# An edge-matrix builder: half-width one-hot products in the inner loop, and weighted copies on GpSimd in fewer, wider operations

## The reference, cut to what matters

```python
h = relu(layernorm(x)); x = x + sage(h, src, dst)          # mean over incoming edges, two convolutions
h = relu(layernorm(x)); x = x + gcn(h, edge_weight, ...)    # weighted sum over incoming edges
h = relu(layernorm(x)); x = x + interaction(h, edge_attr)   # sum over incoming edges, layer norm, three-layer MLP
h = relu(layernorm(x)); x = x + maxk(h, ...)                # top 32 of 256 features, mean over incoming edges
```

## Time and profile before

| | |
|---|---|
| median of 3 runs | 1709.41 us (1706.76 to 1711.73) |
| the profiled execution: time, span | 1709.9 us, 1708.1 us |
| granted TensorE clock over the span | 0.971 of full speed |
| busy over the span: PE, DVE, ACT, POOL | 93%, 56%, 37%, 19% |

### The profile page before, as it was taken

How to read it: one execution, slowest core, us unless ns; L and a number is a source line. 1 busy time by engine, 2 the same in 40 slices (tenths; PEclk the granted TensorE clock), 3 DMA queues, 4 the chain that set the end, 5 groups by cost and what they waited for, 6 DMA issues and landing times.

```text
span 1708.1 us, 41810 instructions
## 1 busy us (share of the span) xinstructions
PE 1587.9 (93%) x11011; PEld 1227.7 (72%) x11012; DVE 960.3 (56%) x2841; ACT 625.3 (37%) x1718; POOL 326.2 (19%) x926
## 2 busy tenths in 40 slices
PE   2899999999988999899999999999899999977996
PEld 1555565555666777588878888888778888855885
DVE  5788888888842222233336666666537777773111
ACT  6677787777721111111112222222234444430000
POOL 1565565655610000000000000000011111110000
PEclk8899999999999999999999999999999999988998
DMA  4266676757696666333355655566322212211444
GB/s 133 70 179 170 156 193 164 186 155 195 163 255 202 193 193 194 127 120 130 122 161 155 178 160 159 163 179 174 108 82 80 76 64 80 80 39 62 150 153 152
DMA packets 353541, 245.55 MB, mean 144 GB/s; under 512 B 195243, under 2 KB 337383, under 8 KB 353511
## 3 DMA queue, kind: packets, MB, share of 16 engines
q1 hardware_dynamic: 353510, 245.19, 50.1%
HBM read 138.17 MB, written 99.31 MB: 139 GB/s over the span
## 4 chain that ended last, share of the span: by engine, by line
issue 60%; PE 33%; DVE 3%; POOL 2%; DVEq 1%; SPq 0%; POOLq 0%; DMA 0%; ACT 0%
PE ps L1377 21%; PE ps L1466 8%; POOL work L643 2%; PE ps L1420 1%; PE ps L1418 1%; DVE e_buf L997 0%; DVE work L943 0%; PE ps L1412 0%; PE ps L1639 0%; SPq L419 0%; PE ps L1353 0%; DVE small L1253 0%; PE ps L1365 0%; DVE e_buf L1013 0%; PE ps L1370 0%
## 5 line engine op out<-in xcount | busy, mean ns | idle before, releaser
L1466 PE MATMUL ps<-arena 128*128 128x256 f16 (+1 forms) x5000 | 605.3, 274 | 18.3 <-DVE arena L1317 8.9
L1466 PEld LDWEIGHTS ps<-arena 128*128 128x128 f16 x5000 | 488.1, 98 | 115.5 <-issue 47.2
L1377 PE MATMUL ps<-e_buf 128*128 128x400 bf16 (+1 forms) x2476 | 374.8, 308 | 23.6 <-DVE e_buf L997 23.5
L1377 PEld LDWEIGHTS ps<-e_buf 128*128 128x128 bf16 x2476 | 217.6, 98 | 169.6 <-DVE e_buf L997 51.6
L1460 PE MATMUL ps<-arena 128*128 128x256 f32 x1250 | 279.6, 381 | 0.6 <-ACT arena L791 0.6
L1460 PEld LDWEIGHTS ps<-arena 128*128 128x128 f32 x1250 | 236.5, 191 | 32.3 <-ACT arena L791 0.9
L628 POOL TENSOR_SCALAR e_buf<-e_buf,w_col 128x128 bf16<-128x128 bf16 x600 | 220.9, 382 | 162.5 <-DVE e_buf L993 156.1
L643 POOL TENSOR_TENSOR work<-work 128x256 f32<-128x256 f32 x75 | 54.4, 726 | 1000.7 <-ACT work L836 1000.7
L997 DVE TENSOR_SCALAR e_buf<-iota,off_g,front 128x400 bf16<-128x400 f16 (+1 forms) x619 | 222.3, 405 | 35.0 <-PE ps L1377 30.6
L993 DVE TENSOR_SCALAR e_buf<-iota,front 128x128 bf16<-128x128 f16 x419 | 111.4, 273 | 40.5 <-PE ps L1377 26.8
L669 ACT ACTIVATE e_buf<-e_buf,front 128x128 bf16<-128x128 bf16 x219 | 88.3, 403 | 106.8 <-DVE e_buf L993 106.4
(11 more groups left out here) (214 smaller groups left out, 1580.4 us busy)
## 6 DMA issues: line engine op xcount, KB each, us to landing
arena<-turned_blocks SPq DMA_DIRECT2D x75, 800.0 KB, 4.3
wgt_blocks<-arena SPq DMA_DIRECT2D x25, 1600.0 KB, 10.3
arena<-wgt_blocks SPq DMA_DIRECT2D x25, 1600.0 KB, 8.3
cnt_blocks<-work SPq DMA_DIRECT2D x25, 800.0 KB, 5.6
turned_blocks<-arena SPq DMA_DIRECT2D x25, 800.0 KB, 3.5
e_raw<-edge_features_padded SPq DMA_DIRECT2D x25, 576.0 KB, 7.8
edge_features_padded<-in_edge_attr SPq DMA_DIRECT2D x24, 512.0 KB, 9.9
out<-arena SPq DMA_DIRECT2D x24, 128.0 KB
```

The costliest lines, as they stand in the source:

```text
L1377: return pe.matmul(bank[:, 0:wide], rows_, cols, start=start, stop=True, skip_group_check=True)
L1466: m = pe.matmul(agg[par][:, 0:wide], BLK16[par][:, b * P:(b + 1) * P], ZH[zin(i)][:, b * ZW + part * D:b * ZW + part * D + wide], start=(b ...
```

## The change

The loop over remaining tiles goes over pairs of a tile and a half of the columns (`halves`). The table holds where a group's range begins and ends in such pairs, and whether the first remaining tile reaches only into the second half (`only_b`); if so, the loop goes in steps of two, over second halves alone, otherwise over both halves of each tile. A pass multiplies 200 columns. Its set and its Q stand in a ring of four slots that turns with every pass (`slot_of`), so that VectorE may be three passes ahead; slot, tile and half are computed from the pass's number. The set kept for the next group is found in the same way (`kept`).

GpSimd makes the three weighted copies of a middle set by one `tensor_tensor` of 128 x 384, a set read three times, times three factors that are spread over 128 columns each; the copy to `w_col` and the drain fall away. It also walks the loop over remaining tiles and makes their third weighted copy with a `tensor_tensor` of 128 x 128; ScalarE makes only the second. Four operations are added to the table's computation.

```diff
-RINGW = (Q_AT + 2 * HW + 4 * GW + 1) // 2
+RINGW = (Q_AT + 2 * HW + 2 * GW + SLOTS * HW + 1) // 2
...
-PREP_STEPS = PREP_SCAN + 8 * 1 + 17 + 3
+PREP_STEPS = PREP_SCAN + 10 + 19 + 3
...
+        ring_rest = ring[:, REST_AT:REST_AT + SLOTS * SETS].rearrange("p (s a n) -> p s a n", a=4, n=P)
+        ring_q = ring[:, Q_AT + 2 * HW + 2 * GW:Q_AT + 2 * HW + 2 * GW + SLOTS * HW].rearrange("p (s n) -> p s n", n=HW)
...
-        def rest_set(i, part):
-
-            at = REST_AT + i % SLOTS * SETS + part * P
-            return ring[:, at:at + P]
+        def next_sets(par, part, many):
+
+            at = par * SETS + part * P
+            return ring[:, at:at + many * P]
+
+        def rest_set(slot, part):
+
+            return ring_rest[:, slot, part, :] if isinstance(slot, int) else \
+                ring_rest[:, bass.ds(slot, 1), part, :].rearrange("p o n -> p (o n)")
...
-        def q_rest(par):
-            at = Q_AT + 2 * HW + (2 + par) * GW
-            return ring[:, at:at + GW]
+        def q_rest(slot):
+            return ring_q[:, bass.ds(slot, 1), :].rearrange("p o n -> p (o n)")
+
+        def slot_of(e, k):
+            return e.snap(k & (SLOTS - 1), min_val=0, max_val=SLOTS - 1)
+
+        def tile_of(e, it):
+            return bounded(e.snap(it >> 1), 0, ET)
+
+        def half_of(e, it):
+            return bounded(e.snap((it & 1) * HW), 0, HW)
...
-        def end_of(e, v):
-            return bounded(e.snap(v & 511), 1, ET + 1)
+        def halves(e, v):
+
+            lo = bounded(e.snap(v >> 10), 0, 2 * ET + 1)
+            hi = bounded(e.snap(v & 1023), 2, 2 * ET + 2)
+            by = bounded(e.snap((lo & 1) + 1), 1, 2)
+            return e.Fori(lo, hi, by)
...
-            def weigh_pair(c, i, v):
+            def weigh_pair(c, i, rest, v):
                 n, par = c * PER + i, i % 2
-                w = w_col[:, par, :]
-                pool.tensor_copy(w, col[:, C_W0:C_W2 + 1, bass.ds(low_of(pool, v), 1)].rearrange("p a o -> p (a o)"))
-                pool.drain()
+                factors = col[:, C_W0:C_W2 + 1, bass.ds(low_of(pool, v), 1)].broadcast_to([P, 3, P])
+                plain = next_set(par, 0).rearrange("p (o n) -> p o n", o=1).broadcast_to([P, 3, P])
                 wait(pool, s_hotS, n + 1)
                 pool.sem_inc(s_made, 1)
-                for k in range(3):
-                    m = pool.tensor_scalar(next_set(par, k + 1), next_set(par, 0), w[:, k:k + 1], 1.0,
-                                           ALU.mult, ALU.mult)
-                m.then_inc(s_hotP, 1)
-
+                pool.tensor_tensor(next_sets(par, 1, 3).rearrange("p (a n) -> p a n", n=P), plain, factors, ALU.mult
+                                   ).then_inc(s_hotP, 1)
+                k_reg = step_of[mybir.EngineType.Pool]
+                with halves(pool, rest) as it:
+                    k = pool.snap(k_reg, min_val=0, max_val=1 << 20)
+                    t, slot = tile_of(pool, it), slot_of(pool, k)
+                    wait(pool, s_restS, k + 1)
+                    pool.tensor_tensor(rest_set(slot, 3), rest_set(slot, 0), one(col[:, C_W2, :], t).broadcast_to([P, P]),
+                                       ALU.mult).then_inc(s_restP, 1)
+                    pool.reg_add(k_reg, k_reg, 1)
...
-                packed = pairs_of(pool, mybir.EngineType.Pool, c, "fixed")
+                packed = pairs_of(pool, mybir.EngineType.Pool, c, "both")
                 for i in range(PER):
-                    weigh_pair(c, i, packed[i])
+                    weigh_pair(c, i, packed[i], packed[PER + i])
...
-                with act.Fori(high_of(act, v), end_of(act, v)) as t:
+                with halves(act, v) as it:
                     k = act.snap(k_reg, min_val=0, max_val=1 << 20)
+                    t, slot = tile_of(act, it), slot_of(act, k)
                     wait(act, s_restS, k + 1)
-                    act.activation(rest_set(i, 2), rest_set(i, 0), ACT.Copy, scale=one(col[:, C_W1, :], t))
-                    act.activation(rest_set(i, 3), rest_set(i, 0), ACT.Copy,
-                                   scale=one(col[:, C_W2, :], t)).then_inc(s_restA, 1)
+                    act.activation(rest_set(slot, 2), rest_set(slot, 0), ACT.Copy, scale=one(col[:, C_W1, :], t)
+                                   ).then_inc(s_restA, 1)
                     act.reg_add(k_reg, k_reg, 1)
...
+                tiles_under(last_a[:, o], 1, 2 * nb, ALU.is_le)
...
-            chain(dve.tensor_scalar(end, last, 1.0, None, ALU.add))
-            chain(dve.scalar_tensor_tensor(out=pair, in0=rest, scalar=512.0, in1=end, op0=ALU.mult, op1=ALU.add))
+            chain(dve.tensor_tensor(only_b, rest, last_a, ALU.is_gt))
+            chain(dve.scalar_tensor_tensor(out=begin, in0=rest, scalar=2.0, in1=only_b, op0=ALU.mult, op1=ALU.add))
+            chain(dve.tensor_scalar(end, last, 2.0, 2.0, ALU.mult, ALU.add))
+            chain(dve.scalar_tensor_tensor(out=pair, in0=begin, scalar=1024.0, in1=end, op0=ALU.mult, op1=ALU.add))
...
-                dve.reg_add(room, k_reg, 1)
-                with dve.Fori(high_of(dve, v), end_of(dve, v)) as t:
-                    wait(dve, s_restused, dve.snap(room, min_val=1, max_val=1 << 20))
-                    edge_rows(rest_set(i, 0), t, s_restS)
-                    dve.tensor_scalar(rest_set(i, 1), iota1[:, 0:P], one(col[:, C_S, :], t), one(col[:, C_W0, :], t),
-                                      ALU.is_equal, ALU.mult)
-                    edge_cols(n, q_rest(par), GW, t, s_restQ)
+                with halves(dve, v) as it:
+                    k = dve.snap(k_reg, min_val=0, max_val=1 << 20)
+                    t, slot = tile_of(dve, it), slot_of(dve, k)
+                    wait(dve, s_restused, k + 1)
+                    edge_rows(rest_set(slot, 0), t, s_restS)
+                    dve.tensor_scalar(rest_set(slot, 1), iota1[:, 0:P], one(col[:, C_S, :], t),
+                                      one(col[:, C_W0, :], t), ALU.is_equal, ALU.mult)
+                    edge_cols(n, q_rest(slot), HW, t, s_restQ, at=half_of(dve, it))
                     dve.reg_add(k_reg, k_reg, 1)
-                    dve.reg_add(room, k_reg, 2)
                 edge_cols(n, q_next(par), GW, u, s_hotQ)
...
-            pe.sem_inc(s_restused, 2)
+            pe.sem_inc(s_restused, SLOTS - 1)
...
+                kept = slot_of(pe, pe.snap(k_reg, min_val=0, max_val=1 << 20) + (SLOTS - 1))
                 wait(pe, s_taken, n + 1)
                 wait(pe, s_hotQ, n * 2 + 1)
-                product(counts, HW, rest_set(i - 1, 0), q_first(par), start=True)
-                product(weights, HW, rest_set(i - 1, 1), q_first(par), start=True)
-                product(weights, HW, rest_set(i - 1, 2), q_first(par))
-                product(weights, HW, rest_set(i - 1, 3), q_first(par)).then_inc(s_used, 1)
-
-                with pe.Fori(high_of(pe, v), end_of(pe, v)):
+                product(counts[:, 0:HW], rest_set(kept, 0), q_first(par), start=True)
+                product(weights[:, 0:HW], rest_set(kept, 1), q_first(par), start=True)
+                product(weights[:, 0:HW], rest_set(kept, 2), q_first(par))
+                product(weights[:, 0:HW], rest_set(kept, 3), q_first(par)).then_inc(s_used, 1)
+
+                with halves(pe, v) as it:
                     k = pe.snap(k_reg, min_val=0, max_val=1 << 20)
+                    slot, at = slot_of(pe, k), half_of(pe, it)
                     wait(pe, s_restQ, k + 1)
-                    product(counts, GW, rest_set(i, 0), q_rest(par))
-                    product(weights, GW, rest_set(i, 1), q_rest(par))
+                    product(span(counts, at, HW), rest_set(slot, 0), q_rest(slot))
+                    product(span(weights, at, HW), rest_set(slot, 1), q_rest(slot))
                     wait(pe, s_restA, k + 1)
-                    product(weights, GW, rest_set(i, 2), q_rest(par))
-                    product(weights, GW, rest_set(i, 3), q_rest(par)).then_inc(s_restused, 1)
+                    product(span(weights, at, HW), rest_set(slot, 2), q_rest(slot))
+                    wait(pe, s_restP, k + 1)
+                    product(span(weights, at, HW), rest_set(slot, 3), q_rest(slot)).then_inc(s_restused, 1)
                     pe.reg_add(k_reg, k_reg, 1)
 
                 wait(pe, s_hotQ, n * 2 + 2)
-                product(counts, GW, next_set(par, 0), q_next(par))
+                product(counts[:, 0:GW], next_set(par, 0), q_next(par))
                 wait(pe, s_hotP, n + 1)
-                product(weights, GW, next_set(par, 1), q_next(par))
-                product(weights, GW, next_set(par, 2), q_next(par))
-                product(weights, GW, next_set(par, 3), q_next(par)).then_inc(s_used, 1)
+                product(weights[:, 0:GW], next_set(par, 1), q_next(par))
+                product(weights[:, 0:GW], next_set(par, 2), q_next(par))
+                product(weights[:, 0:GW], next_set(par, 3), q_next(par)).then_inc(s_used, 1)
```

(2 more changed lines are left out.)

18 lines of the change are left out of this document (9 added, 9 removed).

## The result

The changed kernel takes 1984.5 us (median of 4 runs, 1982.9 to 1987.0), the kernel before 1708.1 (4 runs, 1705.3 to 1711.7): 1.162 times as long, 95% interval 1.159 to 1.165. That is 276 us more; 204 were forecast. The profiled execution has a span of 1985.2 us.

What follows compares the result with a forecast made beforehand. The prediction took TensorE's columns and VectorE's instruction stream to bound the build, and TensorE's register steps to bound it after the change. Its sum was 1709.9 + 202 (build) + 2 (table) = 1914 us, range 1840 to 1990.

Steps and rivals of the forecast that it cites:

- What bounds the kernel before: In the build, 426 of 1708 us, TensorE's columns (1.72 us a group) and VectorE's instruction stream were both at the limit.
- whatever the operations take: VectorE in the build: its sequencer needs 1.5 to 1.7 us a group, however long its operations last.
- the busy shares do not show it: In the build, VectorE runs at TensorE's pace, 1.73 us a group, which busy shares were said to hide.
- TensorE's steps decide: In the changed build, TensorE's register steps set the pace: 628 us for 426, +202 us; chance 0.54.
- 24 x 0.10 + 0.1 ... = 2.5 us: TensorE's group in the changed build: 24 register steps at 0.10 us, plus 0.1 for branch and matmuls' hand-over.
- up to 50 ns more, 0.4 us: Upper end for TensorE's eight matmuls a group with addresses in registers: up to 50 ns more each, 0.4 us.
- The estimate of 17 ns a step: TensorE's register steps priced by the skill's issue floor: 24 would take 0.4 us, hidden under columns; the prediction set it aside.
- VectorE, 572 us: VectorE in the changed build: 20 steps and six operations a group at 86 ns; 572 us, below TensorE's 628; rival's chance 0.20.
- 1.0 to 1.1 and 0.36 us: GpSimd's new operations: 384 columns in 0.96 to 1.09 us, a pass's 128 in 0.32 to 0.36, hidden; rival's chance 0.07.
- VectorE's operations get no longer in sum: VectorE in the build: 200 instead of 400 columns saves 0.1 us a pass; 32 more passes cost 0.6 each.
- The clock: Rival: TensorE's clock falls to 1.2 GHz throughout the build, +254 + 2, 1966 us; chance 0.12.
- The columns: TensorE's loop streams 149,600 columns less, 64 us; rival where columns decide: 1648 us, chance 0.05.

Runs made afterwards that it cites:

- the two loops: Kernel before, with a table flag sending second-half-only groups to a second copy of TensorE's loop, 200 columns wide at fixed addresses: 1704.5 us, 0.997.
- the first experiment: Kernel before, with TensorE reading the same remaining-tile sets at addresses computed from its own counter, 20 register steps a group instead of 8: 1816.9 us, 1.064.

## Why the prediction was right, and where its sizes were off

*What bounds the kernel before: right in the main.* TensorE's columns and VectorE at one pace is what the two loops showed: 64 us of columns less, and the build's end moves by 0.2 us. More steps on TensorE alone slow it too. That VectorE's pace there is its steps, "whatever the operations take", is not shown. In the stretch of the earlier trace rows, by the columns of the earlier trace rows, its operations fill 5.08 of 5.20 us:

```profile
293.40:298.60 5.20, 5.20 (x37) 3.12 (x36) 5.08 (x19) 4.96 (x15) 3.53 (x12) 1.00 0.67 177
```

So "the busy shares do not show it" holds for the 353 of 426 us of the whole build, and not there; steps and operations both fit in 1.73 us. Only at 20 steps a group do the runs tell them apart: 2.5 us with VectorE's operations held or not.

*TensorE's steps decide: right.* Without its address steps the changed kernel is 90 us faster; with GpSimd's part undone, or a quarter of the columns gone, it is as slow as it was. Granted clock, VectorE, GpSimd and columns each have room. Of what the prediction named as signs, the unnamed pauses ahead of line 1404 and VectorE waiting for TensorE are there. Two are not: the build takes 702 us, outside the 600 to 650, and the matmuls of a pass are 0.14 us apart, not 0.1. The time lies 5.5 us inside the range's upper end, 1990, so the range held by little.

*The term that was mis-sized* is "24 x 0.10 + 0.1 ... = 2.5 us" a group. It measured 2.9, which is 580 us over 200 groups instead of 500. The further passes and the fp32 work are then 702 - 580 = 122, against 128; that this comes so near is in part luck, as by line 1412's starts a further pass takes 0.3 us more than forecast and the fp32 work behind a round 0.2 less, while the 426 us that the builds here are counted from leave out some 5 us at the ends (479.0 - 47.7 = 431). So the missing 74 us are those of the one-pass group, and most of it is in the eight matmuls whose address is in a register. I priced their steps as the others and put "up to 50 ns more, 0.4 us" at the upper end; it is 0.04 us for each pair of step and matmul by the four starts, 0.3 of the 0.4 us. The upper end was nearer: the row I held it against was VectorE's, and no row of the kernel before has a TensorE matmul behind the step that makes its address.

The estimate of 17 ns a step, worked out from the issue floor of about 20 cycles in the Trainium skill's "Runtime: NRT & Kernel Launch", section Instruction fetch mechanics, is no price of a register step: in the first experiment a step came to 118 ns, which a floor does not rule out.

*VectorE, 572 us:* measured 616 where TensorE's addresses are fixed, an instruction at 94 instead of 86 ns; below TensorE's 702, as said.

*GpSimd:* 837 and 415 ns for 1.0 to 1.1 and 0.36 us. Its time is hidden, as said. "VectorE's operations get no longer in sum" was wrong: line 1020's comparison took 672 ns in the loop, 255 with GpSimd's part undone, and VectorE's busy time in the build rose from 353 to 492 us. It cost nothing behind TensorE's steps, and 45 us in the kernel where these are few. That GpSimd holds VectorE was not among the rivals.

*The clock:* its rival gave 1966 us, nearer to the time than my 1914, so the time alone would have picked it. The runs do not: it had 1.2 GHz throughout, with a granted clock near 0.5 as its sign; the granted clock was 0.92 in the build, and with a quarter fewer columns at 0.68 nothing was gained or lost. *The table:* +2 us, measured 2. *The columns:* saved, and hidden behind the steps.

## What to carry to other kernels

Count register steps per engine and iteration beside the busy time: an engine that is 93% busy at fixed addresses had room for eight steps a group and not for 24. Where a size may take only two values, two copies of the loop with fixed addresses cost a test and a branch a group here and no time in the build, while a computed address cost a step of 0.1 us or more at every matmul that used it. Try each part of a change by itself: GpSimd's operation cost nothing inside the slow kernel and 45 us in the fast one.

## What I had not expected of the hardware

A VectorE comparison of 128 columns went from 0.31 to 0.88 us beside a GpSimd operation of two inputs that started with it. On TensorE a step and the matmul that takes its address from it are 0.14 us, where steps alone are 0.1 apart. GpSimd compares 128 columns (f16 in, bf16 out) in 630 ns and copies as many with a factor in 369. With the granted clock at 0.68 over 707 us and a quarter fewer columns the kernel was as slow as at 0.92 with all of them.
